# A two-layer attention and feed-forward kernel: the hardware loops of TensorE and ScalarE written out as straight code

## The reference

```
x = x + L0_xattn(layernorm(x), ctx)   # 32 heads of 128, 8 key/value heads, biases, softmax, output projection
x = x + L0_ffn(layernorm(x))          # relu(x up)^2 down + (x fc1 expert) * (sum of top-2 logits) fc2, then layernorm
x = x + L1_xattn(layernorm(x), ctx)   # rmsnorm first; 32 heads of 16, 8 key/value heads
x = x + L1_ffn(layernorm(x))          # 8 experts relu(x We + be), mean of the 2 that the gate picks
```

## The kernel before

| phase | PE | ACT | DVE | POOL, SP |
|---|---|---|---|---|
| first attention, steps 4 to 27 | 3 passes of 8 steps | 3 of 8 | 3 of 8 | loops of 3 |
| first feed-forward, chunks 1 and 2 | 2 of 1 | 2 of 1 | 2 of 1 | none |
| second attention | steps 2 to 13: 3 of 4 | steps 2 to 13: 6 of 2 | steps 2 to 13: 12 of 1 | loops over tiles |

## Time and profile before

### The profile page before, as it was taken

One profiled execution on the slowest core, in us unless ns is written; L12 is line 12 of the kernel. 1 busy time (PEld: TensorE's weight loads), 2 busy tenths in 40 slices (PEclk: granted clock), 3 DMA queues, 4 the chain that ended last, 5 costly groups with the idle time before them and its releaser, 6 DMA issues. The chain is left out here.

```text
span 1905.6 us, 36270 instructions
## 1 busy us (share of the span) xinstructions
PE 1791.0 (94%) x14128; PEld 986.8 (52%) x14128; DVE 1237.0 (65%) x2288; ACT 901.1 (47%) x1433; POOL 496.5 (26%) x370
## 2 busy tenths in 40 slices
PE   5989999999999999999999999887999999999997
PEld 2545555555555555555555444444555555555553
DVE  5785564656556555656565677668678677777862
ACT  5544344343434434443434333244667566666652
POOL 0161823506116052084000000000223223323324
PEclk9989999999999999999999999998999999999999
DMA  5011221301204012033101100013000000000000
GB/s 227 23 45 46 95 83 35 111 2 67 78 1 144 1 65 82 1 133 123 57 1 50 67 1 1 0 63 159 7 7 12 8 7 7 13 7 7 7 12 12
DMA packets 18378, 88.82 MB, mean 47 GB/s; under 512 B 2608, under 2 KB 2864, under 8 KB 10160
## 3 DMA queue, kind: packets, MB, share of 16 engines
q1 hardware_dynamic: 18224, 86.58, 12.6%
HBM read 65.60 MB, written 20.97 MB: 45 GB/s over the span
## 5 line engine op out<-in xcount | busy, mean ns | idle before, releaser
L642 PE MATMUL bank<-R 128*128 128x512 f16 (+1 forms) x7152 | 1309.2, 342 | 22.5 <-DVE X L1574 6.6
L642 PEld LDWEIGHTS bank<-R 128*128 128x128 f16 x7152 | 585.2, 99 | 662.9 <-issue 43.3
L1489 DVE SCALAR_TENSOR_TENSOR R<-bank,biases,R 128x512 f16<-128x512 f32 x288 | 204.7, 746 | 251.2 <-ACT R L1094 209.3
L505 POOL TENSOR_TENSOR R<-R 128x512 f32<-128x512 f32 x112 | 157.1, 1402 | 451.3 <-ACT R L1285 450.1
L1094 ACT ACTIVATE R<-bank,biases 128x512 f16<-128x512 f32 x128 | 87.8, 686 | 235.5 <-PE bank L642 234.8
L396 POOL TENSOR_SCALAR R<-R 128x2048 f32<-128x2048 f32 (+1 forms) x20 | 34.0, 1698 | 436.0 <-PE bank L642 377.1
L1285 ACT ACTIVATE R<-R,msk 128x512 f32<-128x512 f32 x128 | 90.3, 716 | 57.6 <-DVE R L1823 57.5
L642 PE MATMUL bank<-CT,R 128*128 128x512 f16 x384 | 93.7, 396 | 17.0 <-DVE CT L1463 11.7
L1574 DVE SCALAR_TENSOR_TENSOR X<-bank,X 128x512 f32<-128x512 f32 x128 | 86.8, 683 | 34.7 <-PE bank L642 34.6
L1501 DVE SCALAR_TENSOR_TENSOR R<-bank,R 64x512 f16<-64x512 f32 x64 | 44.0, 687 | 99.5 <-ACT R L1102 99.1
L1823 DVE SCALAR_TENSOR_TENSOR R<-bank,R 128x512 f32<-128x512 f32 x128 | 86.9, 680 | 30.4 <-PE bank L642 29.6
(11 more groups left out here) (148 smaller groups left out, 2026.4 us busy)
## 6 DMA issues: line engine op xcount, KB each, us to landing
R<-in_wB SPq DMA_DIRECT2D x16, 1024.0 KB, 5.6
R<-in_wX SPq DMA_DIRECT2D x16, 1024.0 KB, 4.9
w_split<-AW SPq DMA_DIRECT2D x16, 1024.0 KB, 4.8
R<-w_split SPq DMA_DIRECT2D x12, 1024.0 KB, 7.0
R<-in_ctxT SPq DMA_DIRECT2D x4, 1024.0 KB, 10.1
X<-in_x SPq DMA_DIRECT2D x4, 1024.0 KB, 14.1
out<-X SPq DMA_DIRECT2D x16, 256.0 KB, 2.0
R<-in_wB SPq DMA_DIRECT2D x7, 512.0 KB, 5.7
```

Source lines behind the costliest of these rows:

```text
L505: g.tensor_tensor(acc, acc, tmp[:, e % 2, :], ALU.add).then_inc(e_acc, 1)
L642: last = pe.matmul(dst, a(sa), b(sb_), start=(k == 0), stop=(k == m - 1))
L1489: v.scalar_tensor_tensor(out=dst, in0=src, scalar=bias, in1=hi, op0=ALU.add, op1=ALU.subtract).then_inc(done, 1)
```

## The change

Six of the hardware loops are replaced by Python loops, which emit the same steps one after another with constants in place of registers: all three of PE, all three of ACT, and one of the three of DVE (the feed-forward chunks). DVE keeps its loops over the steps of the first attention (line 1682) and of the second (line 2015), and POOL and SP keep theirs.

```diff
@@ -817,7 +817,7 @@
-            with pe.Fori(0, 3) as i:
+            for i in range(3):
                 for k in range(8):
@@ -1044,13 +1044,13 @@
             ffn_chunk(0)
-            with pe.Fori(1, NC - 1) as c:
+            for c in range(1, NC - 1):
                 ffn_chunk(c)
...
-            with pe.Fori(0, 3) as i:
+            for i in range(3):
...
@@ -1227,7 +1227,7 @@
-            with act.Fori(0, 3) as i:
+            for i in range(3):
                 for k in range(8):
@@ -1427,11 +1427,11 @@
-            with act.Fori(1, NC - 1) as c:
+            for c in range(1, NC - 1):
                 ffn_chunk(c)
...
-            with act.Fori(0, 6) as i:
+            for i in range(6):
                 for k in range(2, 4):
                     attn_step(i * 2 + k, k % 2)
@@ -2008,7 +2008,7 @@
-            with dve.Fori(1, NC - 1) as c:
+            for c in range(1, NC - 1):
                 ffn_chunk(c)
```

## The result

The changed kernel takes 1894.52 us (median of 5 runs, 1893.27 to 1895.68) where the kernel before takes 1903.72 us (5 runs, 1902.93 to 1906.93). The ratio is 0.9947, with a 95% interval of 0.9933 to 0.9962, so it is faster, by half a per cent: 9.2 us between these medians, 10.1 us by the ratio. The prediction was 1895.0 us, 10.74 us less than the 1905.76 us it started from.

The account below looks back on a forecast made before the run. PE, busy 94% of the span, bounds the kernel. Of its stalls' 13.96 us, 3.22 us stay through DVE's branch, so 10.74 us off 1905.76 us gives 1895.0 us; range 1890.2 to 1900.4 us.

Parts of the forecast that it names:

- The four stalls of PE, 13.96 us: PE's loop branches, two in each attention: 4.42, 2.58, 3.64 and 3.32 us, all removed by the change.
- DVE's branch, uncovered: First attention, steps 12 and 20: DVE's kept branch, hidden before by PE's idling, now costs 1.63 + 1.59 = 3.22 us.
- one-for-one step: First attention step with DVE's addition to X 1.05 us late lasted 1.04 us longer than usual, so no slack.
- The first stall with PE's name as DVE's releaser: DVE's wait behind its first branch names PE; equal lateness (1.63, 1.59 us) says DVE's stream was late anyway.
- ACT, registers, short loops: 0: ACT's eight branches, PE's and ACT's register instructions, and DVE's one-step second-attention loop: taken as 0 us gained or lost.
- The clock: Rival: PE's 1.6 us idling at DVE's two branches lowers its clock, 1.7 us more each: 1898.5 us; chance 0.10.
- The change doesn't do what it says: Rival: PE's stalls belong to refilling its instruction store, not the branch; time stays 1905.8 us; chance 0.05.
- Straight code starves: Rival: newly straight code arrives late, ten packets at 1.6 us each, 16 us: 1911 us; chance 0.05.
- its first half: Loop bodies that were kept must now be brought in, such as PE's second feed-forward chunk, three packets.
- ScalarE's part: ACT's later steps of the second attention, 12 steps of 40 activations, need some seven packets more.
- the straight steps show no issue stall: Argument against starving: straight steps before and after the loops have no issue stall.

Follow-up runs that it names:

- the loops of one pass: Changed kernel, but TensorE's first and second attention code stands in six hardware loops of one pass each, no branch going back: 1894.9 us, ratio 0.9938.
- padded kernels: Changed kernel with 129 or 258 instructions that only count a semaphore added in VectorE's straight steps 1 to 3: 1897.05 and 1897.32 us.
- VectorE's short loop: Changed kernel with VectorE's first-attention loop straight and its one-step loop over the second attention straight too: 1889.47 us; with only the former straight 1889.76 us.
- ScalarE-only kernel: Kernel before with ScalarE's three loops straight, TensorE's and VectorE's kept: 1904.21 us against 1906.08 us, ratio 0.9988.
- 95 and 223: Changed kernel with 95 semaphore-counting instructions ahead of VectorE's loop: 1888.9 us; with VectorE's first pass straight, loop two passes, body 223 records later: 1890.88 us.

## Why the prediction was right

**The four stalls of PE, 13.96 us.** Right in place and cause. All four are gone in the changed kernel, with PE's edit alone they go too, and the loops of one pass show that it was the way back and not a branch as such. In the profiled pair the second attention gave back 3.64 + 3.32 = 6.96 us as predicted.

**DVE's branch, uncovered.** Right: the steps came down to 31.83 and 31.71 us where 31.68 and 31.64 were forecast, so this term was 1.79 + 1.67 = 3.46 us and not 3.22. DVE's lateness itself was 0.1 to 0.2 us longer than before (8.61 and 8.49 us after the V projection in place of 8.45 and 8.41), and it went into the steps one for one: less the usual 6.82 us these are 1.79 and 1.67 us. The first attention gave back (34.47 - 31.83) + (32.63 - 31.71) = 3.56 us in place of 3.78, and the sum became 10.52 in place of 10.74 us. The one-for-one step read from the earlier trace rows was the key: it said that there was no slack, at a place where no row of PE showed a wait in a usual step. That the uncovered stall is DVE's branch was shown by opening that loop. These tenths are within what changes from execution to execution: on the padded kernels' chip the changed kernel's two steps had 31.69 and 31.62 us, an excess of 1.65 + 1.58 = 3.23 us.

**The first stall with PE's name as DVE's releaser.** Its length was a better witness than the name, as the kernel with VectorE's loop alone opened shows (0.26 us).

**ACT, registers, short loops: 0.** Nothing was found for registers (one-pass loops) and for VectorE's short loop. For ACT the four steps agree (147.01 and 147.06 us); the 1.9 us between the medians of that run stand in no row of its loops.

**The clock.** The rival's price was paid in neither step: both have 1.00. The prediction's reason for the 1.7 us at the first way back, that PE idled longer there, doesn't hold: in the ScalarE-only kernel PE idled 3.01 us at that place in place of 2.68, and the step had 1.00, while a step of the second attention had 0.92. The four places together lost the same there (and 0.9 us more in the kernel with VectorE's loop alone opened), so the sum of 13.96 us held better than its terms. What decides when the clock falls stays open.

**What the sum doesn't hold, and luck.** The spans of the two profiled executions differ by 12.2 us. The V projection of step 11 already starts 1.3 us earlier (421.02 and 419.73). The difference arises ahead of the loops, in code that no edit touched, between the V projections of steps 1 and 2:

```profile
109.94:148.70 38.76, 35.42 (x269) 20.50 (x268) 28.07 (x33) 18.57 (x25) 23.44 (x16) 0.92 0.22 80
...
110.14:147.15 37.01, 34.22 (x270) 20.31 (x269) 27.47 (x33) 18.73 (x27) 22.73 (x16) 0.96 0.18 62
```

The first is the kernel before, the second the changed one, and the clock is 0.92 and 0.96. Such parts come and go from execution to execution. So the medians' 9.2 us, the ratio's 10.1 us, and 11.2 us between the medians on the padded kernels' chip (1905.12 and 1893.96) scatter around the 10.52 us of the four places. That the forecast of 1895.0 us came within 0.5 us of the measured time is in part luck: it started from 1905.76 us, the median of three executions, where five have 1903.72.

**The rivals.** "The change doesn't do what it says" fell with the one-pass loops. "Straight code starves" fell by the absence of issue waits, though its first half happened: code that had been kept is brought in now. Between 1148 and 1240 us, in the feed-forward phase, the kernel before moved no packet of instructions; this is the changed kernel's answer for the same stretch:

```profile
q8 instruction: 4, 0.07, 0.3%
q14 instruction: 2, 0.02, 0.1%
```

Six packets, and nobody waited. ScalarE's part was near the estimate too: with its loops alone opened q14 moved 40 packets in place of 34, six more where the prediction put some seven. The prediction's word that the straight steps show no issue stall has the one exception named above, 1.7 us, in both kernels.

## What to carry to other kernels

Look for idle time with "issue" behind it at the points where a long hardware loop goes back, and price it from the distance between two equal groups, against the same distance in a usual pass: the idling alone was 2.68 us of 4.42. Before taking it as won, look at which other engine's loop goes back at the same moment and how much slack its chain has: a late step elsewhere in the trace may show that it has none, as it did here. Opening the loops of the slowest engine alone uncovered the next; opening both, or moving the second one's body, brought the rest.

## What the runs showed of the hardware

A way back of VectorE to the same body of 8 steps, 342 records in the trace, either costs about 1.7 us of issue or nothing, by where the body stands in the instruction stream: shifts of 0, 129 and 258 instructions stalled, 95 and 223 didn't. That is what blocks of 128 instructions would give, since 0, 129 and 258 leave 0, 1 and 2, and 95 and 223 both leave 95. Blocks of 64 or 32 would fit these five shifts as well; the packets speak for 128. The queue q14 moves packets of 8 KB (0.33 MB in 40), half of PE's q8 (1.84 MB in 112), and q8 brings 2 x 14128 matmuls and weight loads in 112 packets, 252 to a packet besides the register instructions. And 129 and 258 more instructions on VectorE brought q14 to 41 and 42 packets from 40.

q14 carries the code of VectorE and of ScalarE: from the kernel before, its 34 packets fall to 26 when VectorE's loop over the first attention alone is opened, and rise to 40 when ScalarE's loops alone are, while q8 stays at 120.

The Trainium skill ("Runtime: NRT & Kernel Launch", section Instruction fetch mechanics) has a store of two blocks of 256 instructions for most engines, and a stall when the target of a taken branch lies outside the two. The second half agrees with the runs: VectorE's stall comes with three packets and its absence with none. The first doesn't, if a record is one instruction: a body of 342 lies within two blocks of 256 for two places in three, and two places that are 129 apart can't both miss, yet shifts of 0 and 129 both stalled. How many blocks are kept stays open.

ScalarE's body in the first attention is of similar length (347 records) and didn't stall. In the kernel with VectorE's loop alone opened ScalarE goes back too, and q14 brings no packet between 420 and 430 us, so its code was still at hand. Whether only its place spared it wasn't tried.

An instruction that only counts a semaphore takes VectorE about 0.1 us (4.24 us for 43), so padding has to stand where the engine is idle.
